# Softmax attentions of a decoder: one pool of three PSUM banks for scores and side products, the longest returned taken next

## The chip, the cores and the metric

The kernel runs on one core of one Trainium2 chip. A core has TensorE (matmuls, with weight loads that the profile calls PEld), VectorE (DVE), ScalarE (ACT), GpSimd (POOL) and SyncE (SP, which mostly issues DMAs). Each engine works off its own queue in order, and they wait for one another by semaphores. Matmul results land in PSUM, eight banks of 2 KB per partition; another engine must read a bank before the next product may overwrite it. The metric is the device time of one launch in microseconds (us).

## The reference

A two-layer decoder on x of shape (4, 512, 256), with a context of (4, 1601, 128). Every sublayer's result is added to x and normalized. Layer 0: causal linear attention, then a causal softmax attention plus a softmax attention over the context (16 heads of 16), then grouped experts. Layer 1: a state-space scan, then two blocks with softmax attention (16 heads of 32: one over x, masked after the softmax, one over the context), each with a small MLP, then a gated feed-forward. What the change touches is only the softmax attentions:

```python
# layer 0, both attentions share the sum y
att = jnp.einsum('bhqd,bhkd->bhqk', q, k) * scale
att = jnp.where(causal[None, None], att, -jnp.inf)
y = jnp.einsum('bhqk,bhkd->bhqd', jax.nn.softmax(att, axis=-1), v)
attc = jnp.einsum('bhqd,bhkd->bhqk', qc, kc) * scale
y = y + jnp.einsum('bhqk,bhkd->bhqd', jax.nn.softmax(attc, axis=-1), vc)
# layer 1, in each block; causal in the first
a = jax.nn.softmax(jnp.einsum('bhsd,bhtd->bhst', q, k) * D ** (-0.5), axis=-1)
if causal:
    mask = (jnp.arange(t)[None, :] > jnp.arange(s)[:, None]).astype(a.dtype)
    a = a * mask
o = jnp.einsum('bhst,bhtd->bhsd', a, v)
```

## The kernel before, in words

The program is a row of stages. Three of them are softmax attentions, all made by `softmax_attention`: the mixed attention (tag `mx`, 32 jobs; a job is four heads of one batch against own or context keys), the first block (`a1`, 16 jobs) and the second (`a2`, 16 jobs). In the profile the tiles of both blocks are called `a_...`.

A job is worked in these steps. "stack": TensorE makes a projection (q, or a cut of k) in a bank; "split": ScalarE writes its high part (`qh`, `kh`, line 878 or 884), VectorE the low part (`ql`, `kl`, lines 927 and 932), which returns the bank, and DMAs lay them into slots. "peak": products of keys and queries (line 790) whose maxima VectorE takes (line 940). "tops" and "turn_tops": the maxima are turned by TensorE (line 801), and "tops_turned" copies them out of the bank (VectorE, line 958, in `mx`; ScalarE, line 915, in the blocks). "weigh": for a block of 128 keys and two heads, two score products (line 815), which ScalarE turns into exponentials (line 898), each returning its bank. "values": products of the exponentials with the values (line 848). Two "weigh" steps make a block of keys; I call one of them a half-step.

`attention_steps` writes the order of all steps out once, by rules that count half-steps; after each "weigh" come one or two peaks, and in some half-steps a side product: a stack (`stack`), `turn_tops`, or a step of the stage's own, such as turning x, making values (`own`, `context`, `value`) or the product with the output weights (`finish`). Each engine then gets its part of every step in that order. Nothing is reordered later.

Banks. Peaks have three banks (two pairs of banks in `mx`). Scores have a ring of two: banks 4 and 5 in `mx`, 3 and 4 in the blocks. Side products have bank 7 alone (`misc`); before and after the steady part, marked by two "steady" steps, the stage's own products rotate over all three (`wide`). A `Ring` hands out its banks in turn, without regard to when they came back. `take` notes who has the bank and how often it was taken, `empty` is what TensorE waits for before it writes (the bank returned so often), `frees` is the return, attached to the instruction that reads the bank last.

Of the kernel before, what the change touches and what calls it, by code (L numbers as in the profile page):

```python
# [64 lines left out]
class Flag:  # L65

    def __init__(self, nc, ctx, name, step=1):
        self.sem, self.step, self.sent, self.fenced = ctx.enter_context(nc.semaphore(name)), step, 0, 0
# [9 lines left out]
class Bank:  # L79

    def __init__(self, nc, ctx, tile, name):
        self.tile, self.freed, self.takes = tile, Flag(nc, ctx, f"bank_freed{name}"), 0

class Ring:
# [3 lines left out]
    def take(self):  # L90
        self.taken += 1
        return self.slots[(self.taken - 1) % len(self.slots)]

def in_step(items, parts, apart):
# [8 lines left out]
class Decoder:  # L104
# [49 lines left out]
        return self.took[unit][0].tile  # L154

    def frees(self, *unit):
        return self.took[unit][0].freed.up()

    def freed(self, *unit):
        bank, use = self.took[unit]  # L160
# [350 lines left out]
    def attention_steps(self, jobs, q_slots, k_slots, tiled, before, during, beside, at_once, after, rate, lead, urgent):  # L511
# [15 lines left out]
        def side(group):  # L527
            for step in group:
                done.add(step)
                yield step  # L530

        def split(now):

            for kinds in (("stack",), ("split", "tops_turned"), ("turn_tops",), ("tops_turned",), STEPS):
                for at in sorted(due):
                    for step in [step for step in due[at] if step[0] in kinds and (at <= half or now and kinds != STEPS)]:
                        due[at].remove(step)
                        used = any(other[0] in ("split", "tops_turned") for steps in due.values() for other in steps)
                        if step[0] == "turn_tops" and used:  # L540
                            due[half + 1].append(step)
                            continue
                        if step[0] in ("stack", "turn_tops"):
                            follow = ("split", *step[1:3]) if step[0] == "stack" else ("tops_turned", step[1])
                            due[half if now else half + 1].append(follow)
                        yield step
# [58 lines left out]
            yield then,  # L605
        for group in during:
            yield from side(group)
        yield "steady",
        while found < total[0]:
            yield from peaks(found + 8, 8, True)  # L610
            yield from stack()
# [50 lines left out]
        while any(due.values()):  # L662
            half += 1
            yield from split(False)
        yield "steady",
        for group in after:
            yield from side(group)

    def softmax_attention(self, scope, tag, D, scale, jobs, cut_room, q_slots, k_slots, tiled, order, beside):
# [16 lines left out]
        def slot_made(i):  # L686
            eng, name = ((v, "k_slots_made_dve"), (g, "k_slots_made_pool"))[i % 2]
            for r, at in enumerate(base):
                row = 3 * D // 32 * 32 + at
                eng.memset(kst[i][row:at + full].bitcast(F32), -1.0).then_inc(*up(name, i, r))  # L690
                eng.wait_ge(*has(name, i, r))

        def q_slot_made(i, eng):
            name = "q_slots_made" if i else "q_slot_made"
            for at in base:
                row = 3 * D // 32 * 32 + at
                eng.memset(qst[i][row:at + full].bitcast(F32), 0.0).then_inc(*up(name, i))
                eng.wait_ge(*has(name, i))
# [9 lines left out]
                for i in range(2)]  # L708
        turned = sb("mt", [2 * HG, T], F32R)
        a_banks = Ring(self.banks[0:3] if tiled == 1 else self.twins)  # L710
        b_banks = Ring(self.banks[3:5] if tiled == 1 else self.banks[4:6])
        misc, wide = Ring(self.banks[7:8]), Ring([*b_banks.slots, self.banks[7]])
        d_banks, n_banks = Ring(self.banks[5:6]), Ring(self.banks[6:7])
        if pairs:
            sums = [sb(f"pair{i}", [P, T]) for i in range(HG)]
# [44 lines left out]
        def pe_part(part, n, *at):  # L760
            job, qs = jobs[n], qst[n % q_slots]
            nkb = -(-job.nk // P)
            if part == "stack":
                ci, rest = at
                unit = ("q", n) if ci is None else ("k", n, ci)
                k0, w = (0, T) if ci is None else job.cuts[ci]
                if job.first and rest == 0:
                    for event in job.q_after() if ci is None else job.k_after():
                        pe.wait_ge(*event)
                    self.take(misc, *unit)  # L770
                    pe.wait_ge(*self.empty(*unit))
                if job.first:
                    one = job.q if ci is None else job.k(k0, w)
# [4 lines left out]
            elif part == "peak":  # L778
# [7 lines left out]
                bank = self.take(a_banks, part, n, *at)  # L786
                banks = [bank] if tiled == 1 else [bank[:, r, :] for r in range(tiled)]
# [6 lines left out]
                        m = pe.matmul(banks[r][:, P * i:P * i + P], self.identb[:, :], neg_a[:, :], start=False, stop=True)  # L794
                m.then_inc(*self.fills(part, n, *at))
            elif part == "turn_tops":
                bank = self.take(misc, part, n)
                pe.wait_ge(*self.empty(part, n))
                pe.wait_ge(*has("tops_made", n))
                for i in range(TB):  # L800
# [3 lines left out]
            elif part == "weigh":  # L804
                kb, half = at
# [3 lines left out]
                    pe.wait_ge(*has(f"peak{n % q_slots}", n))  # L809
                heads = (2 * half, 2 * half + 1)  # L810
                for h in heads:
                    bank = self.take(b_banks, part, n, kb, h)
                    pe.wait_ge(*self.empty(part, n, kb, h))
                    r0 = base[h % tiled]
                    m = pe.matmul(bank[0:kp, q0:T], ks[r0:r0 + full, h // tiled, k0:k0 + kp],  # L815
                                  qs[r0:r0 + full, h // tiled, q0:T], start=True, stop=job.mask != "causal")
                    if job.mask != "causal":
                        m.then_inc(*self.fills(part, n, kb, h))
# [4 lines left out]
            elif part == "values":  # L823

                kb, half = at
# [26 lines left out]
            elif part == "weights":  # L852
                kb, = at
# [215 lines left out]
                                  ).then_inc(*self.lands(f"peak{n % q_slots}", n))  # L1069

        self.spare = wide
        for part, *at in order():
            if part == "first slot":
                slot_made(0)
                if tiled == 1:
                    q_slot_made(0, v)
            elif part == "rest":
                rest_made()
            elif part == "steady":  # L1080
                self.spare = misc if self.spare is wide else wide
            elif part in ATTENTION:
                for engine in (pe_part, act_part, dve_part, pool_part, sp_part):
                    engine(part, *at)
            else:
                for engine in beside:
                    engine(part, *at)
# [1342 lines left out]
```

## Time and profile before

| | us |
|---|---|
| median of 3 runs | 4054.76 |
| lowest, highest | 4044.93, 4060.32 |
| profiled execution, first to last instruction | 4044.2 |
| TensorE busy | 3511.0 (87%) |
| VectorE busy | 2255.6 (56%) |
| ScalarE busy | 1681.3 (42%) |
| GpSimd busy | 983.5 (24%) |

The page has one time for the profiled execution, its span of 4044.2 us; the runs' times lie between 0.7 us and 16 us above it. An engine's busy time is the union of its instructions' times.
### The profile page before, as it was taken

To read this page: it belongs to the slowest core of one execution; us is meant where nothing else is said; L and a number is where in the kernel's file an instruction comes from. 1 tells how busy PE (TensorE), PEld (TensorE's weight loads), DVE (VectorE), ACT (ScalarE), POOL (GpSimd) and SP (SyncE) were. 2 spreads that over 40 slices of the span, in tenths; PEclk is the share of its full clock that TensorE was granted. 3 is DMA by queue.
4 is the path that set the end of the run, shared out by engine and by line. 5 is a ranking of instruction groups with operands and counts; after the bars stand their busy time and mean duration, and the time that the engine had idled before them with its cause. 6 is when DMAs were issued, how large, how long until landed. Compare 5 with 4: busy or idle time off the path is not lost. (4 is left out here: it accounts for less than half of the span.)

```text
span 4044.2 us, 59055 instructions
## 1 busy us (share of the span) xinstructions
PE 3511.0 (87%) x22156; PEld 2135.3 (53%) x22156; DVE 2255.6 (56%) x4065; ACT 1681.3 (42%) x3067; POOL 983.5 (24%) x1030
## 2 busy tenths in 40 slices
PE   6779999999999884788877689999999996899998
PEld 3433443444443772444546545555555545787877
DVE  6747667577573337544426567676676624534432
ACT  1125646556456231333434135545555553322222
POOL 1200100000000103233333335555555462200000
PEclk9868989999899996898989789999999997999999
DMA  1011211212110311353322244443443402122211
GB/s 68 12 39 45 63 36 45 60 45 51 49 44 23 143 62 42 56 77 62 59 46 76 48 58 63 62 65 56 65 60 58 61 14 77 49 84 63 64 59 61
DMA packets 144627, 229.42 MB, mean 57 GB/s; under 512 B 40916, under 2 KB 90840, under 8 KB 141400
## 3 DMA queue, kind: packets, MB, share of 16 engines
q1 hardware_dynamic: 129048, 216.21, 25.4%
q10 hardware_dynamic: 15296, 9.45, 1.2%
q8 instruction: 177, 2.90, 0.3%
q14 instruction: 106, 0.87, 0.1%
HBM read 99.39 MB, written 8.91 MB: 27 GB/s over the span
## 5 line engine op out<-in xcount | busy, mean ns | idle before, releaser
L940 DVE TENSOR_REDUCE a_mp<-bank 128x1 f32<-128x384 f32 (+2 forms) x1280 | 704.7, 592 | 443.9 <-PE bank L790 429.8
L898 ACT ACTIVATE a_p<-bank 128x512 f32<-128x512 f32 (+1 forms) x1088 | 594.8, 595 | 595.5 <-PE bank L815 523.4
L898 ACT ACTIVATE mx_p<-bank 128x512 f32<-128x512 f32 (+3 forms) x1088 | 548.9, 557 | 471.2 <-PE bank L815 256.2
L940 DVE TENSOR_REDUCE mx_mp<-bank 128x2 f32<-128x768 f32 (+4 forms) x640 | 596.6, 956 | 233.7 <-PE bank L790 143.0
L976 POOL TENSOR_TENSOR a_pair<-a_p 128x512 f32<-128x512 f32 x384 | 491.4, 1310 | 462.0 <-ACT a_p L898 462.0
L790 PE MATMUL bank<-a_ks,a_qs 126*128 126x384 f32 (+2 forms) x1280 | 438.9, 410 | 63.8 <-issue 26.3
L815 PE MATMUL bank<-a_qs,a_ks 128*128 128x512 f32 (+1 forms) x1088 | 421.9, 452 | 41.4 <-DMA a_qs<-a_mt 20.5
L815 PE MATMUL bank<-mx_qs,mx_ks 64*128 64x512 f32 (+3 forms) x1088 | 344.7, 477 | 21.0 <-DMA mx_qs<-mx_mt 13.4
L790 PEld LDWEIGHTS bank<-a_ks,a_qs 126*128 126x128 f32 x1280 | 248.9, 196 | 215.7 <-issue 108.1
L201 POOL TENSOR_TENSOR rs<-ve,neghalf 128x4 f32<-128x4 f32 (+2 forms) x80 | 78.0, 976 | 1168.2 <-DVE ve L196 1125.2
L790 PE MATMUL bank<-mx_ks,mx_qs 62*128 62x384 f32 (+4 forms) x1280 | 314.2, 429 | 7.4 <-DVE mx_mp L940 6.8
L815 PEld LDWEIGHTS bank<-a_qs,a_ks 128*128 128x128 f32 (+1 forms) x1088 | 193.1, 191 | 211.8 <-ACT a_p L898 95.7
L815 PEld LDWEIGHTS bank<-mx_qs,mx_ks 64*128 64x128 f32 (+1 forms) x1088 | 152.1, 193 | 228.4 <-ACT mx_p L898 143.2
L848 PE MATMUL bank<-mx_p,mx_vc 128*17 128x256 f32 (+1 forms) x3328 | 265.9, 393 | 0.0
L848 PE MATMUL bank<-a_p,a_v 128*32 128x256 f32 (+2 forms) x3840 | 263.9, 386 | 0.0
L790 PEld LDWEIGHTS bank<-mx_ks,mx_qs 62*128 62x128 f32 x1280 | 142.8, 198 | 111.0 <-issue 72.5
L983 POOL TENSOR_TENSOR mx_rec<-mx_raw,mx_rec 128x512 f32<-128x512 f32 x16 | 20.3, 1271 | 704.3 <-DMA mx_rec<-mx_flat 704.3
L997 POOL TENSOR_TENSOR a_cut<-a_p,a_upper 128x128 f32<-128x128 f32 x256 | 115.2, 459 | 297.4 <-ACT a_p L898 295.5
L848 PEld LDWEIGHTS bank<-a_p,a_v 128*32 128x32 f32 (+1 forms) x3840 | 99.9, 110 | 113.5 <-issue 65.0
L2164 DVE TENSOR_TENSOR sf_wl<-sf_raw,sf_wh 128x1024 fp32r<-128x1024 f32 x64 | 78.2, 1222 | 141.4 <-ACT sf_wh L2156 141.3
L222 PE MATMUL bank<-a_yn,a_wk 128*128 128x256 f32 (+2 forms) x256 | 99.2, 495 | 18.9 <-DVE a_ql L927 18.9
L848 PEld LDWEIGHTS bank<-mx_p,mx_vc 128*17 128x17 f32 (+1 forms) x3328 | 55.9, 96 | 107.1 <-issue 94.8
(311 smaller groups left out, 5580.1 us busy)
## 6 DMA issues: line engine op xcount, KB each, us to landing
sf_raw<-in_h_w SPq DMA_DIRECT2D x64, 512.0 KB, 3.5
a_ks<-a_kh SPq DMA_DIRECT2D x96, 192.0 KB, 4.5
ex_w<-in_L_ffn_w SPq DMA_DIRECT2D x16, 1024.0 KB, 5.0
a_qs<-a_qh SPq DMA_DIRECT2D x64, 256.0 KB, 6.1
mx_ks<-mx_kh SPq DMA_DIRECT2D x192, 48.0 KB, 2.1
a_ks<-a_kl SPq DMA_DIRECT2D x48, 192.0 KB, 5.2
mx_qs<-mx_qh SPq DMA_DIRECT2D x128, 64.0 KB, 2.2
mx_rec<-mx_flat SPq DMA_DIRECT2D x128, 64.0 KB, 2.0
```

The source lines that it names most:

```text
L201: g.tensor_tensor(rs[0:np_, 0:n], ve[0:np_, 0:n], self.neghalf[0:np_, 0:n], ALU.pow).then_inc(*self.up("root", *key))
L222: m = self.nc.tensor.matmul(out, l, r, start=k == 0, stop=k == len(pairs) - 1)
L790: m = pe.matmul(banks[r][:, 0:w], qs[r0:r0 + full - 2, j, P * i:P * i + P], ks[r0:r0 + full - 2, j, 0:w], start=True, stop=job.mask != "ca ...
L815: m = pe.matmul(bank[0:kp, q0:T], ks[r0:r0 + full, h // tiled, k0:k0 + kp], qs[r0:r0 + full, h // tiled, q0:T], start=True, stop=job.mask ...
L848: m = pe.matmul(num[32 * h:32 * h + job.vw, q0:q1], val, src, start=kb == half == i == 0, stop=last, skip_group_check=True)
L898: act.activation(probs[place % len(probs)][0:kp, q0:T], self.bank(part, n, kb, h)[0:kp, q0:T], ACT.Exp, scale=scale).then_inc(*self.frees( ...
L940: v.tensor_reduce(best[:, tiled * j:tiled * j + tiled, i, ci], bank[:, 0:w] if tiled == 1 else bank[:, :, 0:w], AX.X, ALU.max).then_inc(*s ...
L976: g.tensor_tensor(sums[h][:, :], even[:, :], odd[:, :], ALU.add).then_inc(*up("pair_made", n, kb, h))
L983: g.tensor_tensor(rec[:, :], raw[:, :], rec[:, :], ALU.mult).then_inc(*up("quotient_made", n))
L997: g.tensor_tensor(cut[place % len(probs)][:, :], probs[place % len(probs)][:, P * kb:P * kb + P], kept[:, :], ALU.mult).then_inc(*up("cut_ ...
L2164: v.tensor_tensor(lo[:, :, :], raws[t % 3][:, :, :], hi[:, :, :].bitcast(F32), ALU.subtract).then_inc(*up("weight_low", t))
```

## The change

The two score banks and bank 7 become one `Pool` of three. `take` hands out the bank that was returned longest ago; a bank counts as returned, for this choice, when the program that writes out the instructions comes to its `frees`, not when the chip gets there (the semaphore wait still sees to the latter). Were all three held, the one taken first would be given again. Scores (line 833 after the change, 815 before), stacks, turned maxima and the stage's own side products all take from it, over the whole stage, so the "steady" steps go.

```diff
 class Bank:
         self.tile, self.freed, self.takes = tile, Flag(nc, ctx, f"bank_freed{name}"), 0
+        self.pool = None
+class Pool:
+    def __init__(self, banks):
+        self.idle, self.held = list(banks), []
+        for bank in banks:
+            bank.pool = self
+
+    def take(self):
+        bank = (self.idle or self.held).pop(0)
+        self.held.append(bank)
+        return bank
+
+    def back(self, bank):
+        if bank in self.held:
+            self.held.remove(bank)
+            self.idle.append(bank)
@@ frees
-        return self.took[unit][0].freed.up()
+        bank, use = self.took[unit]
+        if bank.pool and use == bank.takes:
+            bank.pool.back(bank)
+        return bank.freed.up()
@@ attention_steps, in two places
-        yield "steady",
@@ softmax_attention
-        b_banks = Ring(self.banks[3:5] if tiled == 1 else self.banks[4:6])
-        misc, wide = Ring(self.banks[7:8]), Ring([*b_banks.slots, self.banks[7]])
+        side = Pool([*(self.banks[3:5] if tiled == 1 else self.banks[4:6]), self.banks[7]])
@@ stack; turn_tops
-                    self.take(misc, *unit)
+                    self.take(side, *unit)
-                bank = self.take(misc, part, n)
+                bank = self.take(side, part, n)
@@ weigh
-                    bank = self.take(b_banks, part, n, kb, h)
+                    bank = self.take(side, part, n, kb, h)
@@ the stage's own side products use self.spare
-        self.spare = wide
+        self.spare = side
-            elif part == "steady":
-                self.spare = misc if self.spare is wide else wide
```

Every engine has the same instructions in the same order as before (the lines are numbered 18 to 21 higher). What moves is the bank of a product and so the semaphore that it waits for. `bank_freed4` is the semaphore that counts the returns of bank 4; `bank_freed01` and `bank_freed23` are those of the peaks' pairs; in the names `mx_ks4` and the like the number is the slot.

TensorE, mixed attention over context keys, two half-steps without a side product. Before:

```order
L815 MATMUL bank<-mx_qs2,mx_ks4 128x512 [waits bank_freed4,peak2]
L815 MATMUL bank<-mx_qs2,mx_ks4 128x512 [waits bank_freed5]
L790 MATMUL bank<-mx_ks1,mx_qs3 128x384 [waits bank_freed23]
L790 MATMUL bank<-mx_ks1,mx_qs3 128x384
L848 MATMUL bank<-mx_p2,mx_vc1 17x256
L848 MATMUL bank<-mx_p3,mx_vc1 17x256
L848 MATMUL bank<-mx_p4,mx_vc1 17x256
L848 MATMUL bank<-mx_p5,mx_vc1 17x256
L790 MATMUL bank<-mx_ks2,mx_qs3 128x384 [waits bank_freed01,k_stack2,q_stack3]
L790 MATMUL bank<-mx_ks2,mx_qs3 128x384
L815 MATMUL bank<-mx_qs2,mx_ks4 128x512 [waits bank_freed4]
L815 MATMUL bank<-mx_qs2,mx_ks4 128x512 [waits bank_freed5]
```

After:

```order
L833 MATMUL bank<-mx_qs2,mx_ks4 128x512 [waits bank_freed4,peak2]
L833 MATMUL bank<-mx_qs2,mx_ks4 128x512 [waits bank_freed5]
L808 MATMUL bank<-mx_ks1,mx_qs3 128x384 [waits bank_freed23]
L808 MATMUL bank<-mx_ks1,mx_qs3 128x384
L866 MATMUL bank<-mx_p2,mx_vc1 17x256
L866 MATMUL bank<-mx_p3,mx_vc1 17x256
L866 MATMUL bank<-mx_p4,mx_vc1 17x256
L866 MATMUL bank<-mx_p5,mx_vc1 17x256
L808 MATMUL bank<-mx_ks2,mx_qs3 128x384 [waits bank_freed01,k_stack2,q_stack3]
L808 MATMUL bank<-mx_ks2,mx_qs3 128x384
L833 MATMUL bank<-mx_qs2,mx_ks4 128x512 [waits bank_freed7]
L833 MATMUL bank<-mx_qs2,mx_ks4 128x512 [waits bank_freed4]
```

The second pair of scores waited for banks 4 and 5, both filled by the pair before it; now it takes bank 7, and bank 4 from the pair's first head only.

TensorE, second block, a stack (line 222, later 243) and the two pairs of scores behind it. Before:

```order
L222 MATMUL bank<-a2_yn1,a2_wk 128x384 [waits bank_freed7,context_made]
L790 MATMUL bank<-a2_ks5,a2_qs0 128x384 [waits bank_freed1]
L815 MATMUL bank<-a2_qs2,a2_ks1 128x512 [waits bank_freed3]
L815 MATMUL bank<-a2_qs2,a2_ks1 128x512 [waits bank_freed4]
L790 MATMUL bank<-a2_ks5,a2_qs0 128x384 [waits bank_freed2]
L790 MATMUL bank<-a2_ks5,a2_qs0 128x384 [waits bank_freed0]
L815 MATMUL bank<-a2_qs2,a2_ks1 128x512 [waits bank_freed3]
L815 MATMUL bank<-a2_qs2,a2_ks1 128x512 [waits bank_freed4]
L790 MATMUL bank<-a2_ks5,a2_qs0 128x384 [waits bank_freed1]
L790 MATMUL bank<-a2_ks5,a2_qs0 128x384 [waits bank_freed2]
```

After:

```order
L243 MATMUL bank<-a2_yn1,a2_wk 128x384 [waits bank_freed3,context_made]
L808 MATMUL bank<-a2_ks5,a2_qs0 128x384 [waits bank_freed1]
L833 MATMUL bank<-a2_qs2,a2_ks1 128x512 [waits bank_freed4]
L833 MATMUL bank<-a2_qs2,a2_ks1 128x512 [waits bank_freed7]
L808 MATMUL bank<-a2_ks5,a2_qs0 128x384 [waits bank_freed2]
L808 MATMUL bank<-a2_ks5,a2_qs0 128x384 [waits bank_freed0]
L833 MATMUL bank<-a2_qs2,a2_ks1 128x512 [waits bank_freed4]
L833 MATMUL bank<-a2_qs2,a2_ks1 128x512 [waits bank_freed7]
L808 MATMUL bank<-a2_ks5,a2_qs0 128x384 [waits bank_freed1]
L808 MATMUL bank<-a2_ks5,a2_qs0 128x384 [waits bank_freed2]
```

The stack holds bank 7 before and bank 3 now, so two banks are left to the scores in both, and each score product of the second pair waits for the same exponential as before.

TensorE, mixed attention, a stack (line 222, later 243) that follows turned maxima (line 801, later 819) one half-step on. Before:

```order
L815 MATMUL bank<-mx_qs2,mx_ks0 128x512 [waits bank_freed4]
L815 MATMUL bank<-mx_qs2,mx_ks0 128x512 [waits bank_freed5]
L848 MATMUL bank<-mx_p2,mx_vc1 17x256
L848 MATMUL bank<-mx_p3,mx_vc1 17x256
L848 MATMUL bank<-mx_p4,mx_vc1 17x256
L848 MATMUL bank<-mx_p5,mx_vc1 17x256
L222 MATMUL bank<-mx_xt0,mx_Wq 128x256 [waits bank_freed7]
L222 MATMUL bank<-mx_xt0,mx_Wq 128x256
L815 MATMUL bank<-mx_qs2,mx_ks0 128x512 [waits bank_freed4]
L815 MATMUL bank<-mx_qs2,mx_ks0 128x512 [waits bank_freed5]
```

After:

```order
L833 MATMUL bank<-mx_qs2,mx_ks0 128x512 [waits bank_freed7]
L833 MATMUL bank<-mx_qs2,mx_ks0 128x512 [waits bank_freed4]
L866 MATMUL bank<-mx_p2,mx_vc1 17x256
L866 MATMUL bank<-mx_p3,mx_vc1 17x256
L866 MATMUL bank<-mx_p4,mx_vc1 17x256
L866 MATMUL bank<-mx_p5,mx_vc1 17x256
L243 MATMUL bank<-mx_xt0,mx_Wq 128x256 [waits bank_freed7,bank_freed4]
L243 MATMUL bank<-mx_xt0,mx_Wq 128x256
L833 MATMUL bank<-mx_qs2,mx_ks0 128x512 [waits bank_freed4]
L833 MATMUL bank<-mx_qs2,mx_ks0 128x512 [waits bank_freed5]
```

The stack waited for the copy of the turned maxima out of bank 7; now it takes another bank. The first head of the last pair now takes bank 4, which the score product just before it filled, and the second takes bank 5, the one that the turned maxima had.

## Rows read from the trace of the kernel before

**Rows 1.** Windows: busy us (count) per engine, granted clock, DMA share, GB/s.
```profile
701.19:710.31 9.12, 9.09 (x76) 3.72 (x77) 6.99 (x9) 7.01 (x14) 0.00 (x0) 1.00 0.15 35
205.00:1310.00 1105.00, 1027.07 (x7586) 446.79 (x7584) 702.09 (x927) 595.69 (x1174) 70.36 (x61) 0.90 0.19 46
1630.00:2120.00 490.00, 389.23 (x2628) 224.85 (x2628) 216.27 (x413) 184.83 (x344) 164.96 (x314) 0.91 0.39 60
2340.00:3340.00 1000.00, 939.90 (x6864) 544.70 (x6862) 623.13 (x1305) 539.14 (x1013) 531.42 (x426) 0.98 0.38 55
```

**Rows 2.** Line 815 alone: idle of its loads until what (us, times).
```profile
  ACT mx_p L898: 148.8, 381
...
  ACT a_p L898: 113.0, 283
```

**Rows 3.** Timeline, mixed attention: start us, us, engine, line, operation [idle before].
```profile
702.88 0.23 PEld L815 LDWEIGHTS bank<-mx_qs,mx_ks 64*128 64x128 f32 x2
...
703.53 1.09 ACT L898 ACTIVATE mx_p<-bank 128x512 f32<-128x512 f32 x2 [0.67 <-PE bank L815]
...
704.26 0.18 PEld L815 LDWEIGHTS bank<-mx_qs,mx_ks 64*128 64x128 f32 x1 [0.42 <-ACT mx_p L898]
...
704.67 0.18 PEld L815 LDWEIGHTS bank<-mx_qs,mx_ks 64*128 64x128 f32 x1 [0.23 <-ACT mx_p L898]
...
704.86 1.09 ACT L898 ACTIVATE mx_p<-bank 128x512 f32<-128x512 f32 x2 [0.24 <-PE bank L815]
...
705.83 0.35 PEld L815 LDWEIGHTS bank<-mx_qs,mx_ks 64*128 64x128 f32 x2 [0.42 <-ACT mx_p L898]
```

**Rows 4.** Timeline, second block, weight loads of one stalled pair.
```profile
2702.97 0.19 PEld L815 LDWEIGHTS bank<-a_qs,a_ks 128*128 128x128 f32 x1 [0.50 <-ACT a_p L898]
...
2703.45 0.19 PEld L815 LDWEIGHTS bank<-a_qs,a_ks 128*128 128x128 f32 x1 [0.30 <-ACT a_p L898]
...
2704.47 0.19 PEld L790 LDWEIGHTS bank<-a_ks,a_qs 126*128 126x128 f32 x1 [0.72 <-DVE a_mp L940]
```

**Rows 5.** Waits of TensorE, whole span: us in total, times, longest.
```profile
PE bank L222 <- DVE a_ql L927: 29.9, 20, 2.9
...
PE bank L790 <- DVE a_mp L940: 26.2, 24, 2.4
...
PE bank L815 <- ACT a_p L898: 17.3, 51, 1.0
...
PE bank L801 <- DVE a_kl L932: 9.9, 7, 2.2
...
PE bank L222 <- DVE mx_mt L958: 9.4, 11, 1.2
PE bank L222 <- DVE mx_ql L927: 9.3, 6, 1.8
PE bank L801 <- DVE mx_kl L932: 8.8, 9, 1.8
...
PE bank L801 <- DVE a_ql L927: 7.7, 3, 3.1
...
PE bank L815 <- ACT mx_p L898: 5.6, 18, 0.6
```

**Rows 6.** Timeline, second block, a side product behind a stack.
```profile
2695.80 1.08 ACT L898 ACTIVATE a_p<-bank 128x512 f32<-128x512 f32 x2 [0.85 <-PE bank L815]
...
2697.07 0.68 DVE L927 SCALAR_TENSOR_TENSOR a_ql<-bank,a_qh 128x512 fp32r<-128x512 f32 x1
...
2697.80 1.16 PE L222 MATMUL bank<-a_wv,a_yn 128*128 128x128 f32 x8 [1.54 <-DVE a_ql L927]
```

**Rows 7.** Timeline, mixed attention, copy of the turned maxima and the next scores.
```profile
736.17 0.68 DVE L958 CAST mx_mt<-bank 8x512 fp32r<-8x512 f32 x1 [0.85 <-PE bank L801]
...
736.59 1.08 ACT L898 ACTIVATE mx_p<-bank 128x512 f32<-128x512 f32 x2 [1.25 <-PE bank L815]
...
738.04 0.19 PEld L815 LDWEIGHTS bank<-mx_qs,mx_ks 64*128 64x128 f32 x2 [0.33 <-issue]
```

More of the change, by code:

```diff
@@ L664, in attention_steps @@
             yield from split(False)
-        yield "steady",
         for group in after:
```

## The prediction

> **What bounds the kernel now.** I read the busy times by stretch first, one stretch per softmax attention: mixed (205 to 1310 us), first block (1630 to 2120) and second block (2340 to 3340). TensorE is busy 1027.07, 389.23 and 939.90 us in them, VectorE 702.09, 216.27 and 623.13, ScalarE 595.69, 184.83 and 539.14 [rows 1]. So TensorE sets the pace in 2595 of the 4044.2 us, and the change can only bring what TensorE loses there by waiting for one of the three banks. The rest of the program, 1449 us, has no pool and stays.
>
> Next, who holds up the score matmuls (line 815). Their weight loads sat idle until an exponential (line 898) had emptied a bank for 148.8 us in the mixed attention (381 times) and 113.0 us in the blocks (283 times) [rows 2]. By the list of waits the array itself stood still for only 5.6 and 17.3 us of that [rows 5]. Neither number is the loss; the timeline shows it. At 702.88 both loads of a half-step (the scores and exponentials of two heads) start within 0.23 us, and the two products run side by side in two row groups. At 704.26 the first load starts and the second only at 704.67, since the exponential pair begun at 703.53 ended at 704.62 [rows 3]. 0.41 us lie between the loads instead of about 0.05, so such a wait costs 0.36 us, though the array counts as busy. Of the nine weight-load waits on ScalarE from 701.6 to 711.9 four are of this kind; the other five, all of 0.42 us like that at 704.26, only follow the value products, which keep the array busy, and cost nothing. The Trainium skill says as much ("TensorE: Matmul & The Clock Gate", section "Architectural detail"): TensorE's queue can pull weight loads ahead of running matmuls; taken without it, 148.8 us would be called lost, and the trace agrees with the rule by 5.6 us of standstill.
>
> Last, the side products (projections stacked for later jobs, turned maxima, values, residuals). All of them used bank 7 alone, so each waits until the one before has been read. Six rows of the list of waits are of this kind: 29.9 + 9.9 + 9.4 + 9.3 + 8.8 + 7.7 = 75.0 us in 56 waits [rows 5], and this is array standstill. One of them: the values' product of line 222 stands 1.54 us until 2697.80, when VectorE, has made `a_ql` from bank 7 (2697.07 + 0.68) [rows 6].
>
> **The change, part by part.** No engine's order of instructions changes, none is added or removed; only which bank each product takes, and so what it waits for. Dropping "steady" alone does nothing to the order either.
>
> *Scores.* I counted, over the changed order, how many score products back the last use of each bank lies. Before it is two for all but the few first. After, in the mixed attention 578 of 1088 have three, 386 two, 24 one, and 97 follow a side product (3 more lie further back); first block 32, 140, 35 and 49 of 256; second block 228, 482, 17 and 105 of 832. With three, the second head needs the exponential of the half-step's first head and not its second: one exponential earlier, 1.09 / 2 = 0.54 us [rows 3], more than the 0.36 us that a wait costs. Mixed attention: 381 waits x 4/9 = 169 that cost, x 0.36 = 61 us; of its 544 second heads 326 (60%) get three, and they lie where the waits are dense, in half-steps with no side product (all but one of the heads from 701 to 710), so I take 75%: 46 us. Blocks: a stalled pair there starts 2702.97, the second 2703.45: 0.48 us apart where the load itself takes 0.19, about 0.3 a wait [rows 4]. But that very pair keeps its wait: a stack holds the third bank, and it still needs the two exponentials before it, as the second place of the order shows. In the second block 42% of second heads (157 + 18 of 416) and about as many first heads get an older bank, so 283 x 0.4 x 0.3 = 34 us. Together 80 us. Bounds: below, the standstill of 5.6 + 17.3 = 22.9 us; above, all of 148.8 + 113.0 = 261.8 us.
>
> *Side products.* They now take a bank last used by an exponential, most often one half-step back or more. At 2697.80 it would be the bank that the first exponential of the pair at 2695.80 had emptied by 2696.34 (1.08 / 2 later) [rows 6], 1.4 us before VectorE was done. Bounds: nothing, if what comes next on TensorE needs VectorE just as late; 75.0 us at most. I put in all 75, and discount below.
>
> *New waits.* A score product may now wait for a side product's bank, which VectorE returns at its place in its queue, behind reductions; behind that product every later matmul is queued, and behind them the exponentials. The nearest rows: at 735 to 738 the copy of the turned maxima ends at 736.85 and the scores that would take its bank start at 738.04, 1.19 us later; the first head, which would now need the exponential pair ended at 737.67 (736.59 + 1.08), has 0.37 us left [rows 7]. Cost nothing; up to 0.96 us, one reduction, if that cover goes.
>
> *What is late next.* 80 + 75 = 155 us is the gain if nobody else holds TensorE. VectorE does: its reductions (line 940) free the peak banks, TensorE already stands 26.2 us for them [rows 5], and right behind the stalled pair above is one more, 0.72 us of load idle until 2704.47 [rows 4]. VectorE is busy 702.09 / 1105 = 64% and 623.13 / 1000 = 62% of the long stretches. If TensorE, come early, lost its gain each time that VectorE is busy, 37% would be left, 57 us; if never, 155. In the dense stretch of 9.12 us VectorE has 6.99 and ScalarE 7.01 us of work [rows 1], and the three costly waits in it take 1.08 us, which leaves 8.04: both would still follow. I take 0.6, between the two: 0.6 x 155 = 93, rounded to 95 us. Against the profiled execution's span of 4044.2 us that is 3949; the runs' median, 4054.76, lies 10.6 us above the span (what lies around it and the spread of 4044.93 to 4060.32), so 4054.76 - 95 = 3960 us.
>
> **Rivals.**
> *The waits move to VectorE.* The peak matmuls and the turned maxima simply wait longer and TensorE arrives where it did. For it: VectorE's 62 to 64%, the 26.2 us that TensorE stands at line 790 already. Against: VectorE is busy only 44% (216.27 / 490) of the first block. Left would be the 22.9 us at most: 4032 to 4050, 4040 as its middle.
> *The clock comes along.* The granted clock is 0.90, 0.91 and 0.98 in the three stretches [rows 1]; a mean of 0.90 between the levels of 2.4 and 1.2 GHz is 20% of the time at 1.2 GHz: 221 us of the mixed attention, 88 us (18% of 490) of the first block. If fewer standstills turned a quarter of these 309 us to 2.4 GHz, matmul work of 77 us would take 39: 95 + 38 = 133 us gained, 3922 us. For it: the two stretches with most standstill have the low clock. Against: most of it may hang on the long waits for transfers before a job's first scores, which stay. The Trainium skill has this as a rule (same page, "A second HAM failure mode: psum-queue depth-cycling"): short idles between groups that cycle through banks make the clock swing. No row here shows the cause of a single fall.
> *Slower: VectorE's returns end up in the scores' way.* 76 half-steps (24 + 35 + 17) have a first head that needs the exponential just before it, and a second head that needs a side product's bank. If each first head lost a full 0.54 us and each second a reduction of 0.96 us, 76 x 1.5 = 114 us; with the gain of 95 this ends at 4054.76 + 19 = 4074. It decides once VectorE's return comes more than a half-step (1.57 us, 704.26 to 705.83 [rows 3]) after the side product. Against it: the 1.19 and 0.37 us of room.
>
> **How the numbers follow.** The forecast case, 60 to 120 us gained, has 0.62; the clock case, 120 to 155 gained, 0.17; a gain between the forecast and the moved waits, 20 to 60 us, 0.09; moved waits 0.08; slower 0.04. Faster by over 0.5% (20 us, about what a measurement of this kernel tells from no change) is 0.62 + 0.17 + 0.09 = 0.88, same 0.08, slower 0.04. The forecast's own range is 3935 to 3995. With one in ten left out at each side the range is 3905 to 4035.
>
> **What would show it.** Right: the idle of line 815's weight loads until ScalarE falls from 261.8 us to under 170; the six rows of side products fall from 75 us to under 25; busy microseconds of VectorE and ScalarE stay the same; line 790 waits longer for VectorE, at most 60 us more; the mixed attention loses some 50 us of its 1105 and the two blocks 20 each; everything else keeps its length. Wrong: if scores wait for VectorE's or ScalarE's side reads (`a_ql`, `mx_mt`, `a_v`) for over 20 us, the slower case is at work; if 815's waits are gone and the stretches are as long, the waits moved; if the clock of the mixed attention rises above 0.93, the clock case.

## The result and the profile after

| | before | after |
|---|---|---|
| median of 4 runs each, same chip (us) | 4057.54 | 3950.33 |
| lowest, highest | 4044.93, 4061.13 | 3938.57, 3954.17 |
| profiled execution, span | 4044.2 | 3947.2 |
| TensorE / VectorE / ScalarE busy | 3511.0 / 2255.6 / 1681.3 | 3430.7 / 2250.0 / 1677.1 |
| granted clock over the span | 0.923 | 0.928 |

The ratio after to before is 0.9738, 95% interval 0.9715 to 0.9762: 2.6% faster. The forecast was 3960 us with a range of 3905 to 4035.

The stages tell where the time came from. Here a stage lasts from its first peak or score product to its last, read off the trace; the rest of the program is what remains of the span.

| us | before | after | gained |
|---|---|---|---|
| mixed attention | 1101.9 | 1027.9 | 74.0 |
| first block | 494.0 | 477.2 | 16.8 |
| second block | 1032.0 | 1018.8 | 13.2 |
| rest | 1416.3 | 1423.3 | -7.0 |

The rest has the same instructions; its 7.0 us are spread over four pieces, of which the one ahead of the mixed attention has 3.4. Windows over the three stages after (columns as in [rows 1]):

```profile
207.60:1235.50 1027.90, 949.18 (x7563) 411.86 (x7566) 696.72 (x929) 592.25 (x1171) 70.33 (x61) 0.94 0.20 49
1544.80:2021.90 477.10, 390.63 (x2607) 226.84 (x2607) 229.57 (x435) 183.47 (x342) 161.64 (x308) 0.93 0.42 62
2214.50:3233.30 1018.80, 966.13 (x6891) 564.16 (x6891) 653.01 (x1366) 536.88 (x1014) 528.63 (x425) 0.97 0.40 58
```

VectorE and ScalarE do the work they did. Now line 833 (815 before), the idle of the score products' weight loads and what ended it:

```profile
  ACT a_p L916: 68.1, 189
  ACT mx_p L916: 43.3, 107
...
  DVE a_ql L945: 8.4, 13
  DVE mx_ql L945: 3.1, 6
```

The first two rows leave 111.4 us of the 261.8 of [rows 2]; new are the 11.5 us until VectorE's low parts of q. The same half-steps as in [rows 3], weight loads alone:

```profile
663.54 0.26 PEld L833 LDWEIGHTS bank<-mx_qs,mx_ks 64*128 64x128 f32 x2 [0.42 <-issue]
...
664.88 0.19 PEld L833 LDWEIGHTS bank<-mx_qs,mx_ks 64*128 64x128 f32 x2
...
666.27 0.19 PEld L833 LDWEIGHTS bank<-mx_qs,mx_ks 64*128 64x128 f32 x2 [0.42 <-issue]
...
667.43 0.26 PEld L833 LDWEIGHTS bank<-mx_qs,mx_ks 64*128 64x128 f32 x2 [0.42 <-issue]
...
669.05 0.19 PEld L833 LDWEIGHTS bank<-mx_qs,mx_ks 64*128 64x128 f32 x2 [0.42 <-issue]
...
670.32 0.19 PEld L833 LDWEIGHTS bank<-mx_qs,mx_ks 64*128 64x128 f32 x2
```

Both loads of every half-step start together ("x2"). In [rows 3] they lay 0.41 us apart in some half-steps. From the first to the last of these lines are five half-steps in 6.78 us, 1.36 each; before, five at the same place took 1.55 each.

The list of waits, TensorE, whole span (us in total, times, longest):

```profile
PE bank L808 <- DVE a_mp L958: 29.5, 23, 2.7
...
PE bank L819 <- DVE a_mm L970: 20.3, 11, 2.6
...
PE bank L819 <- DVE mx_mm L970: 16.3, 14, 2.3
...
PE bank L808 <- DVE mx_mp L958: 8.9, 19, 1.4
...
PE bank L243 <- ACT a_p L916: 5.0, 13, 0.9
PE bank L819 <- ACT a_p L916: 4.5, 5, 1.1
PE bank L243 <- DVE a_kl L950: 3.9, 2, 3.7
...
PE bank L819 <- DVE mx_kl L950: 3.5, 4, 0.9
...
PE bank L833 <- DVE a_ql L945: 2.6, 3, 1.1
```

Of the six rows of side products in [rows 5], 75.0 us, one is left, `mx_kl` at line 819 with 3.5. A seventh, the prediction's sum did not have it, went from 7.1 to 3.9 us (`a_kl` at line 222, later 243). New is that side products wait for an exponential to be read out of their bank: 5.0 and 4.5 us in the rows shown, 11.5 us in all. `a_ql` has a new row at line 833, 2.6 us: scores that wait for a stack's bank. The turned maxima (line 819) wait longer for VectorE's tops: 20.3 and 16.3 us, where it was 8.7 and 13.2. Line 808's standstill for the peak banks went from 26.2 to 29.5 in the blocks, and its weight loads' idle shows more of it:

```profile
  DVE a_mp L958: 102.6, 158
  DVE mx_mp L958: 55.4, 131
```

Before, these were 91.7 and 35.9 us, so together 158.0 instead of 127.6.

Of the array's own standstill in the mixed attention one wait grew more than any other. The product with the output weights (line 222, later 243) waits for GpSimd, which adds a job's share to `mx_y`. In the window of this stage, before and after:

```profile
PE bank L222 <- POOL mx_y L985: 8.4, 3, 3.4
```

```profile
PE bank L243 <- POOL mx_y L1003: 21.4, 3, 7.5
```

These three waits are 13.0 us longer, and as long in the second profile of the changed kernel (21.4).

### The profile page after: what moved, and what is told of

The parts are those of the page before. It is cut to its first block and busy times, and to the rows that moved or that the text cites. A ratio compares the mean times of both kernels' runs of the same rounds, so it can differ in the third digit from the quotient of the medians.

```text
span 3947.2 us, 59055 instructions
## 1 busy us (share of the span) xinstructions
PE 3430.7 (87%) x22156; PEld 2103.0 (53%) x22156; DVE 2250.0 (57%) x4065; ACT 1677.1 (42%) x3067; POOL 983.4 (25%) x1030
## 5 line engine op out<-in xcount | busy, mean ns | idle before, releaser
L808 PE MATMUL bank<-a_ks,a_qs 126*128 126x384 f32 (+2 forms) x1280 | 444.8, 413 | 80.9 <-issue 33.5
L833 PE MATMUL bank<-a_qs,a_ks 128*128 128x512 f32 (+1 forms) x1088 | 409.3, 447 | 30.8 <-DMA a_qs<-a_mt 17.2
L833 PE MATMUL bank<-mx_qs,mx_ks 64*128 64x512 f32 (+3 forms) x1088 | 292.0, 466 | 21.8 <-DMA mx_qs<-mx_mt 16.0
L808 PE MATMUL bank<-mx_ks,mx_qs 62*128 62x384 f32 (+4 forms) x1280 | 278.8, 413 | 10.7 <-DVE mx_mp L958 8.9
L833 PEld LDWEIGHTS bank<-mx_qs,mx_ks 64*128 64x128 f32 (+1 forms) x1088 | 124.7, 189 | 197.7 <-issue 130.7
L808 PEld LDWEIGHTS bank<-mx_ks,mx_qs 62*128 62x128 f32 x1280 | 131.5, 193 | 117.2 <-issue 60.8
L882 PE MATMUL bank<-a_pair,ones 128*32 128x512 f32 x768 | 119.5, 633 | 2.0 <-POOL a_pair L994 1.9
```

What stands on the lines that cost most here:

```text
L808: m = pe.matmul(banks[r][:, 0:w], qs[r0:r0 + full - 2, j, P * i:P * i + P], ks[r0:r0 + full - 2, j, 0:w], start=True, stop=job.mask != "ca ...
L882: m = pe.matmul(self.bank("den", n)[32 * h:32 * h + 32, :], self.ones[0:src.shape[0], 0:32], src, start=first, stop=kb == nkb - 1, skip_gr ...
```

## The experiments

All ratios are to the kernel before on the same chip, with the 95% interval. Stage lengths come from the profiled execution of each.

### Neither part: both waits put back

Kept are the new banks, put back is the age of the bank waited for: a score waits until the score before last has been read, a side product until the last side product has been read. These waits act in the steady part alone, which two "steady" steps mark again; the lines that do this are left out here.

```diff
@@ take
+        if isinstance(ring, Pool):
+            kind, back = ("score", 2) if unit[0] == "weigh" else ("side", 1)
+            if kind in self.kept and self.steady and len(self.last[kind]) >= back:
+                self.nc.tensor.wait_ge(*self.last[kind][-back])
+            self.last[kind].append((bank.freed.sem, bank.takes))
@@ softmax_attention
+        self.kept = ('score', 'side')
```

> The changed kernel, with both old waits put back on TensorE: each score product waits besides for the return of the score product two before it, each side product for the return of the side product before it. Theory (the gain is these two waits and nothing else): as slow as the kernel before, ratio 0.995 to 1.002, mixed attention 1095 to 1105 us. Rival (banks that rotate, or the clock by chance, give part of it): ratio under 0.99.

Measured: 4054.7 us, ratio 1.0007 [0.9988, 1.0026]; stages 1102.5, 494.5, 1035.6. So the whole gain is the age of the bank that is waited for; what else the change moves (which bank it is, the steps that went) is worth nothing that this interval, 8 us to each side, could tell.

### Only the side products free

The two diffs that follow are against the version with both waits put back.

```diff
-        self.kept = ('score', 'side')
+        self.kept = ('score',)
```

> Only the scores' old wait is put back, side products are free. Theory (scores give more than half of the 107 us, as 80 to 75 in the sum): about 45 us of the gain stay, ratio 0.989; mixed attention about 1070 us, first block 477, second block 1025. Rival 1 (the side products give nearly all, since only their waits were standstill of the array): ratio 0.976, mixed attention 1035. Rival 2 (side products give nothing because VectorE is as late anyway): ratio 0.998.

Measured: 4003.33 us, ratio 0.9892 [0.9864, 0.9920]; stages 1076.7, 482.1, 1019.5: 25.2, 11.9 and 12.5 us less than before. The score loads' waits for ScalarE (line 840 in this kernel) stay, a little longer than in [rows 2]:

```profile
  ACT mx_p L923: 154.5, 408
...
  ACT a_p L923: 118.7, 296
```

In the mixed attention the three rows of side products had 27.5 us [rows 5], and 25.2 came. But its granted clock was 0.93 in this execution, against 0.90 [rows 1], so a part of the 25.2 may be the clock's (more on that below). Beside the version with both waits the two parts can be told apart. First that version, then this one:

```profile
206.70:1309.20 1102.50, 1018.69 (x7563) 446.79 (x7566) 703.09 (x929) 594.64 (x1172) 70.33 (x61) 0.91 0.19 46
```

```profile
204.00:1280.60 1076.60, 1007.89 (x7563) 442.96 (x7565) 701.68 (x929) 594.91 (x1172) 70.41 (x61) 0.93 0.19 47
```

Of the 25.9 us between them 15.1 are standstill of the array (83.8 to 68.7), which is what freeing the side products takes away, and 10.8 are busy time, at a clock of 0.93 instead of 0.91.

### Only the scores free

```diff
-        self.kept = ('score', 'side')
+        self.kept = ('side',)
```

> Only the side products' old wait is put back, scores take the longest returned of three banks freely. Theory: about 60 us of the gain stay, ratio 0.985; mixed attention about 1055 us, first block 494 as before, second block 1027. Rival 1: ratio 0.998. If the two parts do not add up (each alone keeps most of the gain, or neither does), the savings depend on each other.

Measured: 3991.98 us, ratio 0.9856 [0.9834, 0.9878]; stages 1055.3, 490.6, 1024.8: 46.6, 3.4 and 7.2 us less than before. The load waits fall as in the changed kernel:

```profile
  ACT a_p L923: 67.9, 187
...
  ACT mx_p L923: 42.4, 103
```

278 waits (381 - 103) are gone in the mixed attention. At 4 in 9 costly and 0.36 us each that is 44 us; 46.6 came. The window of its mixed attention:

```profile
203.70:1258.90 1055.20, 961.78 (x7563) 415.11 (x7566) 697.92 (x929) 591.93 (x1171) 70.39 (x61) 0.91 0.19 48
```

Beside the 1102.5 us of the kernel with both waits the stage is 47.3 us shorter, and the array's busy time is 56.9 us shorter (1018.69, against 961.78) while its visible standstill is 9.6 us longer, at a clock of 0.91 in both. Behind the longer standstill is GpSimd: the array's waits for `mx_y` went from 7.6 to 19.9 us between these two. So the time of these waits did sit inside "busy": a product that starts late beside another keeps the array counted as busy. The two parts add up: 1.08% and 1.44% are 2.52%, where the whole change gave 2.62% in its own measurement. So the waits put back cost nothing much by themselves either.

### All six banks of the blocks in the pool

```diff
@@ softmax_attention
-        a_banks = Ring(self.banks[0:3] if tiled == 1 else self.twins)
-        side = Pool([*(self.banks[3:5] if tiled == 1 else self.banks[4:6]), self.banks[7]])
+        side = Pool([*(self.banks[0:5] if tiled == 1 else self.banks[4:6]), self.banks[7]])
+        a_banks = side if tiled == 1 else Ring(self.twins)
```

> In the two blocks the three peak banks join the pool: six banks for peaks, scores and side products, the longest returned next; the mixed attention as in the changed kernel. Theory (the second block gained only 13 us because a stack leaves two banks to the scores): a further 20 to 30 us off the second block, ratio to before 0.967. Rival (VectorE's reductions hold the second block): no gain there, or a loss where scores wait for VectorE's reductions: ratio 0.974 to 0.985.

Measured: 3928.66 us, ratio 0.9695 [0.9674, 0.9716]; stages 1033.8, 477.5, 988.3. The mixed attention is built as in the changed kernel; the second block gives another 30.5 us. Its weight loads' waits in the second block, in this order: before, changed kernel, six banks.

```profile
PEld bank L815 <- ACT a_p L898: 84.7, 208, 1.5
...
PEld bank L790 <- DVE a_mp L940: 47.4, 80, 2.7
```

```profile
PEld bank L808 <- DVE a_mp L958: 56.1, 96, 3.2
PEld bank L833 <- ACT a_p L916: 52.8, 139, 1.3
```

```profile
PEld bank L808 <- DVE a_mp L958: 32.3, 54, 2.6
PEld bank L833 <- ACT a_p L916: 28.7, 80, 0.6
...
PEld bank L808 <- ACT a_p L916: 17.0, 60, 0.7
```

Between before and after the waits for exponentials fell by 31.9 us and those for the peaks' maxima rose by 8.7. With six banks both fall, to 45.7 us in the two rows of exponentials and to 32.3 us for the maxima, at the same busy time of VectorE (652.85 us, 653.01 after). So VectorE's work could stay as it is; that three fixed banks wait for it is what the pool of six removes. The clock of the second block is 0.983 with six banks and 0.965 after, to three digits (0.983 and 0.967 in the repeated runs below). At 5 us for 0.01, the slope found below for the mixed attention, some 9 of the 30.5 us may be the clock's, an estimate. The first block was as long as after (477.5 and 477.2 us), at a lower clock (0.90, against 0.93).

### VectorE's maxima in the blocks made lighter, before and after

These two kernels leave out the maximum over half the columns of each peak in the blocks, the one on the kernel before, the other on the changed one.

```diff
@@ peak
-  bank[:, 0:w] if tiled == 1 else bank[:, :, 0:w]
+  bank[:, 0:w // 2] if tiled == 1 else bank[:, :, 0:w]
```

> The kernel before, but in the two blocks VectorE takes the maxima of peaks (line 940) over half the columns only, so its share is lighter and part of the maximum is left out. Both theories: somewhat faster than before, ratio 0.985 to 0.995, by the peak waits that go. It is here to be compared with the next run.

> The changed kernel with the same lighter maxima. Theory (VectorE's reductions take back what the scores gain in the second block): the second block is now 30 us or more shorter than with the light maxima alone, against 13 us with full ones. Rival (the scores' waits there hide behind other TensorE work, so nothing is there to gain): the difference stays at 10 to 15 us.

Measured: 4022.14 us, 0.9938 [0.9917, 0.9960], on the kernel before; 3901.54 us, 0.9633 [0.9611, 0.9655], on the changed one. Blocks of the first: 481.6 and 1015.9; of the second: 456.4 and 987.4. The second block of the two (before, then changed):

```profile
2306.70:3322.60 1015.90, 955.53 (x6890) 559.49 (x6890) 449.91 (x1366) 540.26 (x1015) 528.94 (x425) 0.98 0.40 58
```

```profile
2191.90:3179.30 987.40, 936.69 (x6891) 557.82 (x6891) 451.64 (x1366) 537.53 (x1014) 528.43 (x425) 0.98 0.41 59
```

With VectorE 202 us lighter there, the pool gains 28.5 us in the second block (1015.9 to 987.4), just under the 30 expected, where it gained 13.2, and 25.2 in the first (481.6 to 456.4) where it gained 16.8. So of what the pool could give in the second block a third to a half was taken back by waits for VectorE. It is no sharper because the clock has a share here too: to three digits it went from 0.974 to 0.965 with the full maxima and from 0.979 to 0.985 with the light ones. At 5 us for 0.01, again an estimate, the two gains at an equal clock would be some 18 and 25 us.

### One bank moved from the peaks to the pool

```diff
@@ softmax_attention
-        a_banks = Ring(self.banks[0:3] if tiled == 1 else self.twins)
-        side = Pool([*(self.banks[3:5] if tiled == 1 else self.banks[4:6]), self.banks[7]])
+        a_banks = Ring(self.banks[0:2] if tiled == 1 else self.twins)
+        side = Pool([*(self.banks[2:5] if tiled == 1 else self.banks[4:6]), self.banks[7]])
```

> In the two blocks one of the three peak banks goes to the pool: peaks have two, scores and side products four. Theory (the peak banks are what is short there once the pool is in): second block longer than with three and three, 1030 to 1050 us instead of 1019, weight loads of peaks wait for VectorE 85 us or more instead of 56. Rival (scores are short of banks while a stack holds one): second block 1000 us or less. The six banks of e4 gave 30 us; this tells which side used them.

Measured: 4047.62 us, ratio 0.9996 [0.9984, 1.0009]; stages 1032.0, 509.1, 1089.2. The blocks lose all that the mixed attention gains: the second is 70 us longer than after. Weight loads' waits in the second block:

```profile
PEld bank L808 <- DVE a_mp L958: 195.2, 373, 3.1
```

They are 195.2 us against 56.1 after. The direction is the expected one; the size (1030 to 1050 us, 85 us or more of waits) was put far too low. The peaks need their third bank more than the pool needs a fourth. Of the three ways to share six banks that ran, the one pool of six is the shortest in the second block: 988.3 us, 1018.8 for three and three, 1089.2 for two and four.

### The bank returned last taken first

```diff
@@ Pool.take
-        bank = (self.idle or self.held).pop(0)
+        bank = self.idle.pop() if self.idle else self.held.pop(0)
```

> The pool of three, but the bank returned last is taken next. Theory (the age of the bank is the gain, not their number): every first head waits for the exponential just before it, so all of the scores' gain goes and more: ratio 1.00 to 1.02, mixed attention 1100 to 1140 us. Rival (sharing alone gives the gain): ratio 0.975 to 0.985.

Measured: 4577.27 us, ratio 1.1296 [1.1274, 1.1318]; stages 1332.3, 543.2, 1255.2. I had expected at most 2% slower; this missed by far. The same three banks, the same instructions, and 13% more time. Line 833's weight loads in it:

```profile
  ACT mx_p L916: 287.4, 429
  ACT a_p L916: 144.3, 178
  DVE a_kl L950: 102.8, 83
...
  ACT a_v L1812: 91.8, 142
  DVE mx_kl L950: 85.4, 66
```

and one place in the mixed attention:

```profile
827.12 0.74 DVE L945 SCALAR_TENSOR_TENSOR mx_ql<-bank,cols,mx_qh 128x512 fp32r<-128x512 f32 x1
...
827.91 0.18 PEld L833 LDWEIGHTS bank<-mx_qs,mx_ks 64*128 64x128 f32 x2 [1.65 <-DVE mx_ql L945]
```

The score pair could not start until VectorE had made `mx_ql` (827.12 + 0.74): 1.65 us of idle for the loads, 1.16 us of standstill for the array. This is the mechanism of the slower rival: a return by VectorE, or by ScalarE behind its exponentials, that the scores must wait for. It exists, and the order of choice alone decides whether it acts. It is not the whole of the 13%: the theory's waits for exponentials grew too, to 431.7 us in the two rows above (261.8 before), the three rows of side products' reads are 280.0 us, and the clock of the mixed attention, 230 us longer than before, was 0.81. How the loss divides among the three was not tested. In the changed kernel the same mechanism has 11.5 us of load idle for low parts of q and 0.6 for `a_v`.

### The changed kernel and the six banks once more

The changed kernel again, and beside it, on the same chip, the six banks.

> The changed kernel as it is, on the chip of the next run and for a second trace. If the low clock of the mixed attention hangs on its standstills, it is at 1.2 GHz there for 130 to 180 us again (218 before); if it fell by chance, it may be back near 218. Ratio 0.974, mixed attention 1025 to 1035 us.

> Six banks for the two blocks again, beside the changed kernel on one chip: ratio to before 0.9695, 15 to 25 us faster than the changed kernel, all of it in the second block (988 against 1019 us). If the first run was luck, both are at 0.974.

Measured: 3951.92 us, ratio 0.9747 [0.9721, 0.9773], stages 1033.1, 476.9, 1017.4; and 3926.78 us, ratio 0.9688 [0.9662, 0.9714], stages 1038.8, 480.8, 991.7. The second block again has 25.7 us of difference, and the kernels 25.1. The version with six banks beats both kernels of this case. In the mixed attention of the repeated run of the changed kernel the clock is 0.92, against 0.94 in the first profile, and the stage 5.2 us longer. A clock of 0.92 is 164 us at 1.2 GHz, within the 130 to 180 that were expected. But the six banks, with the same code in this stage, had 181 us beside it (0.91), and the kernel with both waits put back 191: the two groups almost meet, and this does not settle whether the low clock hangs on the waits.

## Why the prediction was right, and where it was not

**The total.** Forecast 3960, measured 3950.33; 95 us were put in, the spans differ by 97.0 and the medians by 107.2.

**Scores.** The count of costly waits (46 us in the mixed attention) came out: 46.6 with the scores alone free. Part of that is luck, since the array's busy time fell by 56.9 us and GpSimd's `mx_y`, on which the prediction had no term, took 12.3 back. In the blocks 34 us were put in and 3.4 + 7.2 = 10.6 came. That a stalled pair with a stack in one bank would keep its wait was right. At the place of [rows 4], after:

```profile
2612.33 0.19 PEld L833 LDWEIGHTS bank<-a_qs,a_ks 128*128 128x128 f32 x1 [0.50 <-ACT a_p L916]
...
2612.82 0.19 PEld L833 LDWEIGHTS bank<-a_qs,a_ks 128*128 128x128 f32 x1 [0.30 <-ACT a_p L916]
...
2614.10 0.19 PEld L808 LDWEIGHTS bank<-a_ks,a_qs 126*128 126x128 f32 x1 [0.98 <-DVE a_mp L958]
```

The two gaps are the 0.50 and 0.30 of [rows 4], and the wait for VectorE behind them has grown from 0.72 to 0.98. With six banks the second of the gaps at this place is 0.17.

**Side products.** All 75 us were put in, and all but 3.5 of them went, for 11.5 us of new waits for exponentials; with the side products alone free 49.6 us came in the three stages. At the place of [rows 6], after:

```profile
2606.45 1.09 ACT L916 ACTIVATE a_p<-bank 128x512 f32<-128x512 f32 x2 [0.85 <-PE bank L833]
...
2607.10 1.16 PE L243 MATMUL bank<-a_wv,a_yn 128*128 128x128 f32 x8 [0.19 <-ACT a_p L916]
```

The values' product stands 0.19 us instead of 1.54 and waits for an exponential's bank, as forecast. What was missed is where the rest went in the first block. Of the rows of [rows 5] it had 31.7 us (14.1 of `a_ql` at line 222, 9.9 and 7.7 at line 801), and 11.9 came. TensorE's standstill for the tops was 7.0 us there before and is 18.7 after: VectorE reduces a job's maxima, and TensorE, come early, stands ahead of the products that turn them. 7.2 us more have no releaser in the list (26.3 before, then 33.5, at line 808). The trace names it: each of these ten waits, before as after, ends 0.09 us after a transfer of the keys' low part into its slot has landed. The longest of them but one:

```profile
1823.51 0.98 SPq L1051 DMA_DIRECT2D a_ks<-a_kl  x1
...
1832.96 1.62 PE L808 MATMUL bank<-a_ks,a_qs 126*128 126x512 f32 x3 [6.62 <-issue]
```

This transfer landed at 1832.87. Under the transfer's own name the list has 5.1 us besides (1.9 before). So in the first block TensorE, come early, stood for the tops and for the peaks' keys: 22.1 us more than before.

**The uniform discount of 0.6.** This is the step that failed, though the sum came out. The mixed attention had 46 + 27.5 = 73.5 us put in and gave 74.0; even without the clock's share (below, some 14) that is 0.8 of it. The blocks had 34 + 47.5 = 81.5 us and gave 16.8 + 13.2 = 30.0, which is 0.37, the end that the prediction had worked out for a TensorE that loses its gain whenever VectorE is busy. By luck the two errors cancelled: 155 x 0.6 = 93 against 104 in the stages. VectorE is busy 64% of the mixed attention and 62% of the second block, so its busy share could not have told them apart. For the second block the list of waits could: of the 26.2 us that TensorE stood for the peak banks of the blocks [rows 5], 23.8 are in the second block, in a stage about as long as the mixed attention, which had

```profile
PE bank L790 <- DVE mx_mp L940: 6.8, 16, 0.9
```

The runs with light maxima and with six banks show that a good part of the second block's loss is at that place. For the first block this row says nothing, 2.4 us; its list had 28.2 us for the keys' transfers and 7.0 for the tops, and there its gain went. The discount is not all of it either: with VectorE's maxima halved the blocks gave 28.5 + 25.2 = 53.7 us, still 0.66 of the 81.5, so the sum itself was too large there. Which of its terms was, no run shows.

**New waits at no cost.** Nearly right. At the place of [rows 7] the copy of the turned maxima now ends at 697.24 and the scores come at 698.75:

```profile
696.56 0.68 DVE L976 CAST mx_mt<-bank 8x512 fp32r<-8x512 f32 x1 [0.85 <-PE bank L819]
...
698.75 0.19 PEld L833 LDWEIGHTS bank<-mx_qs,mx_ks 64*128 64x128 f32 x2 [0.33 <-issue]
```

so the room has grown from 1.19 to 1.51 us, and that behind the exponential pair from 0.37 to 0.69. Scores waited for side reads for 13 us of load idle in all, under the 20 us that would have shown the slower case. The rival's mechanism was real, as the run with the last returned bank shows; what kept it away is the rule that picks the bank returned longest ago, and the prediction had argued this from one place only.

**The clock.** The mark was a clock above 0.93 in the mixed attention, and it stood at 0.94 once and at 0.92 once. Six profiles have the changed kernel's code in that stage: 1027.9 and 1028.7 us at 0.94, 1032.0 at 0.93, 1033.1 and 1033.9 at 0.92, 1038.8 at 0.91, some 3.6 us for 0.01. Three have the waits of before: 1102.5 at 0.91, 1101.9 at 0.90, 1117.5 at 0.88, some 5 us for 0.01. To three digits the clock rose from 0.904 to 0.935, and the slopes are 4.8 and 4.5 us for 0.01, so some 14 of the 74 us would be the clock's, an estimate from these; with the side products alone free, at 0.927, 10 or 11 of the 25.2. The other runs bear the size out: over the whole span the clock of 34 executions of the kernel before is 0.920 in the mean (0.914 to 0.924), at 4052 us, and that of eight of the changed kernel 0.926 (0.923 to 0.931), at 3950 us. Among the 34 the time falls by 23 us for each 0.01, which makes the 0.006 between the means some 14 of 102 us. The scores' 47.3 us against the kernel with both waits, at 0.91 in both, need no such share. So the clock case in its size, 38 us, is out, and a smaller share of it came along. The Trainium skill ("TensorE: Matmul & The Clock Gate", section "A second HAM failure mode: psum-queue depth-cycling") holds that short idles between groups that cycle through banks make the clock swing; the trace agrees in direction (0.88 to 0.91 with the waits of before, 0.91 to 0.94 without them), but not by the array's visible standstill, which was 76.0 us in this stage before and 78.7 after; and no run here shows the cause of a single fall.

**The moved waits.** Line 808's weight loads idle 30.4 us longer for VectorE (up to 60 were expected), and the tops' standstill grew by 11.7 us in the first block and by 3.1 in the mixed attention. The rival's mechanism is a part of what the blocks show; in the mixed attention VectorE's part is small, and the wait that grew is the one for GpSimd (13.0 us).

**The rest.** [rows 2]'s 261.8 us fell to 111.4 (under 170 was forecast), VectorE's and ScalarE's busy time stayed within 5.6 us, the blocks gained 16.8 and 13.2 (20 each forecast), the mixed attention 74.0 (some 50).

## What to carry to other kernels

Count a buffer wait not by whether the array stands but by how far apart two products start that could run side by side; and ask of each buffer how old its last reader is, for with equal banks and equal work the choice ran from 0.974 (longest returned first) to 1.130 (last returned first). Discount a gain stage by stage, by the next waits that stand in the list for that stage and not by the next engine's busy share: where peak banks, tops or transfers were already waited for, a third of the gain came through, in the mixed attention some four fifths. The factor itself is no rule; it was not tested beyond these stages. And when waits come back at another set of buffers, try merging that set before making its reader faster: six banks in one pool gave as much in the second block as taking 202 us of work from VectorE.

## What the runs showed of the hardware

A product that starts late beside another in a different row group leaves no standstill in the profile: in the mixed attention the array's busy time fell by 57 us at an equal clock (0.91) with the same 7563 matmuls. The granted clock of that stage was 0.81 with 253 us of array standstill (the kernel with the last returned bank). In the eleven other profiles, with 69 to 93 us, it lay between 0.88 and 0.94 in no order of the standstill: 0.88 with 75.6 us, 0.94 with 78.7, 0.91 with 93.4.
